# Flamingo block in f32 on one core: a wait on VectorE moved, two units of scores moved ahead, and products with an unread result on TensorE

## The reference, cut to what is computed

```
x = x + tanh(g_xattn) * attention(layernorm(x), ctx, ctx)     # 16 batches of 128 x 512
x = x + tanh(g_ffn) * experts(layernorm(x))                   # router, top 4 of 16 experts, and a shared expert

def attention(q, k, v):           # per batch: 8 heads of 16 rows; the 512 columns are the positions
    qk = einsum('bdm,bdn->bmn', qh, kh) / 4
    return einsum('bmn,bcn->bcm', softmax(qk, axis=-1), vh)
```

## Time and the profile before

| | |
|---|---|
| median of 3 runs | 1156.15 us (1154.73 to 1158.93) |
| the profiled execution | 1152.22 us |
| its span | 1150.5 us |
| busy: PE, DVE, ACT, POOL | 97%, 71%, 46%, 53% |
| mean granted clock of TensorE | 1.00 |

### The profile page before, as it was taken

One profiled execution on the slowest core, in us unless ns is written; L12 is line 12 of the kernel. 1 busy time (PEld: TensorE's weight loads), 2 busy tenths in 40 slices (PEclk: granted clock), 3 DMA queues, 4 the chain that ended last, 5 costly groups with the idle time before them and its releaser, 6 DMA issues.

```text
span 1150.5 us, 21591 instructions
## 1 busy us (share of the span) xinstructions
PE 1114.7 (97%) x5718; PEld 742.8 (65%) x5719; DVE 818.8 (71%) x1162; ACT 525.2 (46%) x1055; POOL 607.0 (53%) x597
## 2 busy tenths in 40 slices
PE   3899999999999999999999999999999999999998
PEld 1334434444443446887888878787888878878887
DVE  6799989998989707674434477666666666649887
ACT  1588888887888841111111134444444444421111
POOL 3245645565555324035777446657575665338762
PEclk9999999999999999999999999999999999999999
DMA  9567776777867307956464345575757657533665
GB/s 238 148 181 203 214 209 175 201 202 210 208 185 179 90 20 280 400 172 233 156 234 153 138 145 175 171 230 173 228 180 216 189 176 225 164 95 107 179 196 183
DMA packets 138944, 214.59 MB, mean 187 GB/s; under 512 B 16145, under 2 KB 61713, under 8 KB 138897
## 3 DMA queue, kind: packets, MB, share of 16 engines
q1 hardware_dynamic: 108124, 131.36, 39.4%
q0 software_dynamic: 18016, 61.88, 16.9%
q10 hardware_dynamic: 12756, 20.77, 5.4%
HBM read 117.48 MB, written 91.75 MB: 182 GB/s over the span
## 4 chain that ended last, share of the span: by engine, by line
PE 53%; POOL 5%; DMA 3%; issue 1%; DVE 0%; ACT 0%; POOLq 0%; DVEq 0%; ACTq 0%
PE score_ps L139 20%; PE score_ps L1676 14%; PE d_ps L1635 8%; PE d_ps L1700 7%; POOL w_split L1174 3%; DMA w_raw<-in_L_ffn_w_down_dram 3%; PE o_ps L1635 3%; POOL w_split L1172 1%; PE d_ps L1690 1%; PE o_ps L1690 1%; POOL w_raw L123 0%; DVE hid L1544 0%; DVE th L1539 0%; ACT th L1301 0%; DVE y_all L1448 0%
## 5 line engine op out<-in xcount | busy, mean ns | idle before, releaser
L703 DVE TENSOR_REDUCE maxima<-score_ps 128x2 f32<-128x1024 f32 x256 | 305.9, 1220 | 38.0 <-PE score_ps L808 30.2
L652 ACT ACTIVATE probs<-sb_ps 128x512 f32<-128x512 f32 x512 | 271.3, 602 | 74.9 <-PE sb_ps L835 74.6
L139 PE MATMUL score_ps<-yn_t,w_split 128*128 128x512 f32 x1056 | 254.6, 397 | 0.0
L1676 PE MATMUL score_ps<-w_split,x_split 128*128 x948 | 248.2, 399 | 1.5 <-POOL w_split L1174 0.9
L139 PEld LDWEIGHTS score_ps<-yn_t,w_split 128*128 128x128 f32 x1056 | 197.0, 188 | 51.3 <-issue 5.1
L1676 PEld LDWEIGHTS score_ps<-w_split,x_split 128*128 128x128 f32 x948 | 171.8, 188 | 36.1 <-issue 3.6
L808 PE MATMUL score_ps<-places,q_stack 48*128 48x512 f32 x512 | 160.4, 475 | 22.4 <-DMA q_stack<-q_dram 16.3
L835 PE MATMUL sb_ps<-q_stack,places 50*128 50x512 f32 x512 | 178.2, 470 | 3.6 <-DMA q_stack<-max_t 2.5
L1172 POOL CAST w_split<-w_raw 128x1024 fp32r<-128x1024 f32 x63 | 67.3, 1069 | 182.8 <-DMA w_raw<-in_L_ffn_w_down_dram 83.0
L1174 POOL TENSOR_TENSOR w_split<-w_raw,w_split 128x1024 fp32r<-128x1024 f32 x63 | 152.7, 2423 | 5.1
L846 PE MATMUL o_ps<-probs,v_t 128*17 128x512 f32 x1024 | 136.5, 605 | 0.6 <-ACT probs L652 0.2
(11 more groups left out here) (151 smaller groups left out, 1193.3 us busy)
## 6 DMA issues: line engine op xcount, KB each, us to landing
xs_dram<-zero SPq DMA_DIRECT2D x1, 20224.0 KB, 58.8
stage<-xs_dram SPq DMA_DIRECT2D x316, 64.0 KB, 2.2
res_dram<-stage ACTq DMA_DIRECT2D x79, 256.0 KB, 2.4
places<-k_dram SPq DMA_DIRECT2D x64, 192.0 KB, 3.6
q_stack<-q_dram SPq DMA_DIRECT2D x64, 192.0 KB, 4.0
k_dram<-places SPq DMA_DIRECT2D x16, 512.0 KB, 2.9
q_dram<-places SPq DMA_DIRECT2D x16, 512.0 KB, 3.8
w_raw<-in_L_ffn_w_gate_dram POOLq DMA_DIRECT2D x16, 512.0 KB
```

Of the source, the lines that this page charges most:

```text
L139: mm = pe.matmul(dst[i], w[:, k, f * P:(f + 1) * P], self.yn_t[:, b, k, t * self.SPAN:(t + 1) * self.SPAN], start=(k == 0 and n == 0), sto ...
L652: act.activation(probs[:, c % 2, head(j)[2], :], sb_ps[:, bank_of_score(s, e), :], ACT.Exp, scale=SCALE).then_inc(exp_done, 1)
L703: dve.tensor_reduce(maxima[q % 2][:, :].rearrange("p (h u) -> p u h", u=8)[:, u, :], sa_ps[:, pair_of_unit(q, g, u), :, :], AX_X, ALU.max) ...
L1676: mm = pe.matmul(gu_ps[j], x_split[j][:, b, k, :], w_split[:, bass.ds(at + (a * 3 * ex.PIECE + k * 2 * FE), 2 * FE)], start=(n == 0), stop ...
```

## The change

It does five things.

On VectorE, `unit` no longer waits for `mlo_done` (the split of the maxima two groups back). The wait for BN_STATS, which stood right behind it and so ahead of unit 0, now stands behind unit 0 and ahead of BN_AGGR, with an increment of a semaphore that nobody reads (`dve_waited`).

On TensorE, `FIRST_ORDER` begins with four S (units 4 and 5 of group 1) and two T, where it began with T, S, S, T; it holds as many of each as before. `keep_clock(n)` multiplies `ident` with itself n times, 128 x 128 in plain f32, into a bank of `sb_ps` that is overwritten later: three times behind each of units 3 to 7 of group 0, twice behind the first `values_and_maxima`, three times behind units 2 and 3 of group 1, and in slot 0 four times ahead of its third step and twice ahead of its fifth. That is 29 products. The wait for `o_cleared` ahead of the slots is gone.

```
-                if u == 0 and not (isinstance(g, int) and g < 2):
-                    dve.wait_ge(mlo_done, g - 1)
...
                 if prepared(s):
                     statistics(q // 2, s.r + 1)
-                    dve.wait_ge(bn_done, 2 * s.r + q // 2 + 3)
                 if has_late(s):
                     last_statistics(batch_late(s), 1 if q == 1 else 0, y_done, batch_late(s) + 1)
-                    dve.wait_ge(bn2_done, batch_late(s) + 1)
                 if s.before(NG - 2):
                     unit(q2, g + 2, 0)
                 if prepared(s):
+                    dve.wait_ge(bn_done, 2 * s.r + q // 2 + 3)
+                    dve.sem_inc(dve_waited, 1)
                     first_variance(2 * s.r + q // 2 + 2, q // 2)
                 if has_late(s):
+                    dve.wait_ge(bn2_done, batch_late(s) + 1)
+                    dve.sem_inc(dve_waited, 1)
                     last_variance(batch_late(s))
...
-            FIRST_ORDER = "TSSTSSTSSTSSTSSTSSCTTOMTTSSSTSTDSTTSLSTTSE"
+            FIRST_ORDER = "SSSSTTSSTSSTSSTSSTCTTOMTTSSSTSTDSTTSLSTTSE"
...
-                for step in order:
+                for at, step in enumerate(order):
+                    if s.known() and g == 0 and at in (2, 4):
+                        keep_clock(4 if at == 2 else 2)
...
+            def keep_clock(n):
+
+                for _ in range(n):
+                    pe.matmul(sb_ps[:, 0, 0:P], ident[:, :], ident[:, :], start=True, stop=True)
+
             for u in range(8):
                 for half in range(2):
                     scores(0, 0, 0, u, half)
+                if u >= 3:
+                    keep_clock(3)
...
             values_and_maxima(0, 0, 0, LAST % 3)
+            keep_clock(2)
             for u in range(2, 4):
                 for half in range(2):
                     scores(1, 1, 0, u, half)
-            pe.wait_ge(o_cleared, 1)
+                keep_clock(3)
             slots(pe, slot)
```

More of the change, by code:

```diff
@@ L250, in gated_block @@
         yn_stored = sem("yn_stored")
-        pool_waited = sem("pool_waited")
+        pool_waited, dve_waited = sem("pool_waited"), sem("dve_waited")
         last_y, last_yn, last_hi, last_lo = (sem(n) for n in ("last_y", "last_yn", "last_hi", "last_lo"))
```

## The result

The changed kernel takes 1165.24 us (median of 4 runs, 1159.82 to 1173.12) against 1156.05 us before (4 runs, 1154.73 to 1158.93), a ratio of 1.0082 [1.0048, 1.0116]: slower, where 1150.6 us were forecast. The profiled execution took 1159.82 us, its span is 1158.1 us, 7.6 us longer than that of before.

A forecast was written before the change was run, and what follows sets the result against it. The prediction took TensorE, busy 97% of the span, as the bound, with VectorE waited for in the attention loop. 1.9 us at the start plus 3.6 us in the loop made 5.5 us: 1150.6 us, range 1147.0 to 1158.0 us.

The forecast's parts named there:

- The start: Up to slot 1's reciprocal: an earlier clock rise on TensorE gains 1.9 us, bounds 0.6 and 2.7 us.
- The price of a product: Products of ident on TensorE: 0.22 us each at the high level; three take 0.65 us, at the low level 1.3 us.
- 0.87 us, and hidden: From unit 3 on, a unit with its products costs TensorE this at the high level, against VectorE's 1.157 us.
- The rival "slower": At the start the products do not raise the clock before the first T: 3.8 us lost, 1156.4 us; chance 10%.
- with the fillers there is no gap: Argument against a clock still low at 32 us: the added products leave TensorE no gaps at the start.
- The loop: Attention loop: moved waits let unit 0 start sooner, 0.18 us x 20 = 3.6 us, bounds 0 and 5.0 us.
- register steps on TensorE: In the loop, put at 0.07 us of the 0.25 us excess a slot, which the moved waits would not remove.
- The new order: Slot 0: two units ahead remove VectorE's 2.08 us stall, worth nothing since it goes to the load of x.
- A clock that goes again: At the start the clock comes late or falls while VectorE waits for x: 1152 to 1153 us; chance 12%.
- The sum: Whole kernel: 1.9 + 3.6 = 5.5 us saved, giving 1150.6 us for the median.
- 0.17 and half of 0.46: Chance of faster by over half a per cent: both parts in full (17%) plus half of the forecast's 46%.

The follow-up runs named there:

- e1_dve_only: The kernel before with only the waits on VectorE moved; median 1152.96 us, ratio 0.9974.
- e2_order_only: The kernel before with only the new FIRST_ORDER of slot 0; median 1155.22 us, ratio 0.9989.
- e5_real_fill: The changed kernel with its 29 products made of real data instead of ident; 1155.50 us, one run.
- e12_real_again: The changed kernel with real data instead of ident in its products, repeated; median 1162.34 us, ratio 1.0052.
- e4_fill_only: The kernel before with only the 23 products of ident ahead of slot 0, old waits on VectorE and old order; median 1161.34 us, ratio 1.0050.
- e6_score_fill: The changed kernel with pairs of halves of group 0's scores in place of the products of ident; 1147.85 us, one run.
- e11_warm_keep: The kernel before with moved waits, new order, 16 real-data products ahead of the first scores and two behind each unit; median 1163.76 us, ratio 1.0077.
- e9_warm_real: The kernel before with moved waits and 16 products of real data ahead of the first scores; 1151.49 us, one run.
- e10_warm_ident: The kernel before with moved waits and 16 products of ident ahead of the first scores; 1157.47 us, one run.

## Why the prediction was wrong

**The start: the failing step.** "If the clock rises after some 5 us, two units have been slow and 1.2 us are lost." It didn't rise: TensorE worked from 20 us on without a gap and stayed at the low level until about 50.5 us. The 5 us had no row behind them; the one row on the clock, 9.6 us of nearly gapless work ahead of its rise, was taken for the worst case. The price of a product is the second error, "three take 0.65 us, and at the low level [...] 1.3 us": the product was priced right and the switches around it were left out, 0.58 us a unit at the low level. At the high level a unit takes 1.29 us and not the "0.87 us, and hidden", so a clock that rose would not have hidden the products either.

The two together give the times. The rival "slower" had the transposes 2.1 us late by products alone; five units with two switches each add 2.9, together 5.0 us, measured 4.9. From there it had 8.7 us to the T; nine switches add 2.6, together 11.3, measured 11.3 (32.01 to 43.30). So T at 43.5 instead of its 38.0, measured 43.30. Of the 9.6 us by which `by_values` is late 1.9 us come back up to the reciprocal of slot 1 (14.8 us instead of 16.7), since the clock rises 2.4 us behind its start and not 8.4. That leaves 7.7 us lost for 1.9 us forecast as won. The mechanism is that rival's, given 10%, which put 3.8 us to it. Its condition, a clock still low at 32 us, was met; "with the fillers there is no gap" was no argument against it.

**The loop: right.** Forecast 3.6 us and 11.74 us a slot; measured 3.3 us and 11.76, and e1_dve_only has it by itself. The gap behind BN_STATS vanished whole; the maximum begins 0.60 us after the start of BN_STATS. The Trainium skill (Perfetto Trace Analysis, Sequencer-only Instruction and DVE / Act Engine Instruction) would have it so: a wait of an instruction that only the sequencer handles holds the decoding behind it, that of a VectorE instruction doesn't. The trace agrees, but no run parts this from the removal of `mlo_done`. The slot gave 0.16 us and not 0.25. The prediction had put the rest down to register steps on TensorE; no run shows what keeps it.

**The new order: right within what can be measured.** Its stall goes to the load of x (3.04 us in e2_order_only), and no gain stands clear of the scatter; half a microsecond at the start can't be excluded. In the changed kernel even that stall was gone, because all else was later.

**A clock that goes again.** This rival isn't what happened in the changed kernel, whose clock hadn't risen. e5_real_fill and e12_real_again show it. Where the clock did rise early, it fell within slot 0, at 42.0 and 44.2 us, and rose late again, at 48.8 and 54.5 us; the eight executions of e12_real_again with such a mark had a mean 3.6 us above before's median.

**The sum.** +7.7 at the start and -3.3 in the loop (-0.2 behind it) make 4.2 us at the last reciprocal; the two medians differ by 9.2 us. The profiled execution of the changed kernel was the shortest of its four, that of before was 3.9 us under its median. What makes the others longer no profile here shows; the experts' waits of TensorE, 1.9 to 9.9 us from profile to profile, are one thing that can. That the start costs some 8 us and the loop gives 3 is shown, and the rest of the 9.2 us is not. In the prediction's chances there is a slip without consequence: 0.17 and half of 0.46 make 0.40, not 0.41.

**Open.** What decides in an execution whether the clock rises at 24 us or at 50 was not found: neither what is multiplied nor a lack of gaps does. Whether the changed kernel's four late executions out of four are chance stays open too: e4_fill_only and e12_real_again have five and four late ones of twelve by the mark, and at those odds (9 of 24) four of four would come about one time in fifty, by my estimate. No version that was repeated is faster by more than 0.3%: moved waits alone have 0.9974 [0.9946, 1.0002], with four products in the gap 0.9973 [0.9949, 0.9997].

## What to carry to other kernels

Price work that is to keep a clock up at the clock it has without it, with the switches at both ends of each group, and compare that with the other engine's period; if it doesn't fit, it delays the chain in every execution, while the clock may not come. Put such work only where the engine idles, and look first for a stretch bound by TensorE that would use the clock: here VectorE and a load set the pace up to `by_values`. A wait behind which an independent instruction can go ahead is worth moving, and edits of one diff are worth timing apart: the waits had won 0.3%, and the products lost about 1%.

## What the runs showed of the hardware

A full 128 x 128 plain f32 product between fp32r scores that share the array costs 0.29 us at each end of its group at the low level and 0.21 us at the high one, besides 0.43 or 0.22 us each. Pairs that have the scores' type and use the array as they do pay nothing of the sort (e6_score_fill).

TensorE stayed at 1.2 GHz through 30 us of work without a gap to speak of (20 to 50 us in the changed kernel, 18 to 52 us in e11_warm_keep), while sixteen full products in a row raised it within 6.7 us (e9_warm_real, e10_warm_ident, e11_warm_keep). The Trainium skill (TensorE: Matmul & The Clock Gate, What's actually happening) says that sustained work raises the clock, and that the point shifts from run to run of one kernel. The second agrees, at 24 and 28 us in two executions of one kernel; for the first the traces of the changed kernel and of e11_warm_keep decide, and differ.

The granted clock reads 1.00 from the start until the first recorded change, also where the records last twice as long: L846's 1.91 and 1.05 us are both under 1.00 in the kernel before. The length of a known product tells the level; the column tells it only after its first change.
